# A fused attention and expert-choice kernel: four waits and fills moved to other places

## The chip, the cores and the metric

The kernel runs on one core of a Trainium2 chip. The metric is the time on the device in microseconds (us), the median of several runs.

## The reference, cut to what matters

x has 8 batches of 1024 rows of 256. The kernel computes a row norm of x, attention on it (16 heads of 16, with a second norm, rotary positions, softmax), and a mixture of 8 experts in which each expert takes its best rows; the three are added.

```python
x = L0_attn_x
xn = _layernorm(x, axis=-1)
x = x + _L0_attn_ref(xn, ...) + _L0_ffn_ref(xn, ...)
# attention, on z = norm(xn) * ln_w + ln_b:
scores = einsum('bhqd,bhkd->bhqk', rope(q), rope(k)) / sqrt(hd)
out = einsum('bhqk,bhkd->bhqd', softmax(scores), v)
return xn + out @ Wo.T + bo
# experts: each takes the K = 256 rows of highest affinity of each batch's 1024
gating, index = top_k(softmax(xn @ gate_w).T, K)
h = silu(x_sel @ Wg) * (x_sel @ Wu)
x_out = zeros.at[b_idx, index].add((h @ Wd) * gating)
```

## The kernel before

**Attention.** For each batch b the function attend of every engine walks through 32 cycles of two steps. A step is one group of four heads, one half of the queries and one block of 128 keys. TensorE makes two rows of scores for a step (line 979) into a ring of three buffers, ScalarE takes the exponential of each (line 767), TensorE multiplies the result with the values (line 993). Into the cycles are sown side jobs of TensorE: norm, projections and so on of the next batch, and the output projection ("wo", line 903) of the batch before, in four quarters. In the last batch, which has no next one, the side jobs are those of LAST_JOBS: wo in cycles 9, 15, 23 and 30, "lists" in 27. VectorE takes the top rows of the experts meanwhile, some operations per cycle (TOPS_OF_CYCLE), orders the lists in cycle 26, and copies o_ps out every fourth cycle (line 1436).

**Weights.** An expert's three weights (wg, wu, wd) are loaded by SyncE in load_weights (line 532), all three on one semaphore, w_in. For expert 0 SyncE issues them in the last batch behind its stores of cycle 12. ScalarE casts each to the high part (high_weights, line 736), VectorE subtracts to get the low part (low_weights, line 1367). In the last batch ScalarE makes cast m behind the exponentials of the second step of cycle WEIGHT_CYCLE[m], and VectorE the subtraction in LOW_CYCLE[m]. The wait of a cast is

```python
act.wait_ge(w_in, WEIGHTS * DMA * (e + 1))
```

so each cast waits for all three loads. Casts of later experts stand in the expert units.

**Expert units.** 32 units (8 experts by 4 pairs of batches). GpSimd gathers rows with an indirect DMA (line 666), TensorE turns them (1059), multiplies gate and up (1072) in four blocks f, ScalarE takes silu (751) and a cast (745), VectorE the product (1384) and a subtraction (1376), TensorE the down product (1084), VectorE scales the rows (1399), and GpSimd adds them to the output with an indirect DMA (677). Units 0 and 1 also finish the last batch's attention: quarter_split (lines 1315, 1452, 1454, 1456) and the projections of its quarters. The reciprocals of the softmax sums come from invert (line 1441), which waits for den_in; for the second half of the last batch it stands in unit 0 behind block 1. SyncE writes its result out and spreads it (spread_rec) for unit 1's quarters, behind a load that waits for unit 0's second split.

**The end.** After its last scatter GpSimd waits for the landing of all scatters (line 725), then every engine ends with a DRAIN and an exchange of semaphores (line 113).

**The start.** VectorE sets constants (lines 1551 to 1555), among them ones in the two v_ones buffers, then norms the first half of batch 0 (norm1, norm2, norm3: lines 1121, 1125, 1130), splits the four attention weights (first_weights, line 1563) which ScalarE casts, and so on; GpSimd fills v_ones (set_v, line 647) after const_set has counted minus_half and both memsets. The bound that decides whether scores need a shift (limits) is told to all engines by bound_ready.

Of the kernel before, what the change touches and what calls it, by code (L numbers as in the profile page):

```python
# [19 lines left out]
DMA = 16  # L20
# [96 lines left out]
def program(nc, ctx, g):  # L117
# [4 lines left out]
    ST = SLOTS // P  # L122
    HALVES = CAP // P
    UNITS = NB * HALVES // ST
# [8 lines left out]
    def sb(name, shape, dt=F32):  # L133
        return ctx.enter_context(nc.sbuf_tensor(name, shape, dt))
# [4 lines left out]
    def sem(name):  # L139
        return ctx.enter_context(nc.semaphore(name))  # L140
# [40 lines left out]
    v_ones = [sb(f"v_ones{i}", [P, KT, HPG, KEYS_W]) for i in range(2)]  # L181
# [59 lines left out]
    scattered = [sem(f"scattered{i}") for i in range(UNITS)]  # L241
# [7 lines left out]
    const_set, weights_split, weights_high = sem("const_set"), sem("weights_split"), sem("weights_high")  # L249
# [27 lines left out]
    rotated, sq_ready, v_peaked, bound_ready = (sem(n) for n in ("rotated", "sq_ready", "v_peaked", "bound_ready"))  # L277
# [76 lines left out]
        return qk[:, k, :] if th == 0 else (rec, num)[k // 2][:, k % 2, :]  # L354

    FIRST_BANKS = tuple(score[i][:, w, :] for i in range(RING) for w in range(2)) + (o_ps[:, :], side[:, :])
    WEIGHT_CYCLE = (20, 21, 22)
    LISTS_CYCLE = 26
    LOW_CYCLE = (28, 29, 30)
    END_BANKS = {("wo", q): (q // 2, q % 2) for q in range(QUARTERS)}  # L360
    ROUTER_CYCLE = (9, 19)
    SPLIT_CYCLE, LAST_SPLIT_CYCLE = (7, 8, 17, 18), (7, 8, 14, 18)
# [30 lines left out]
    def hold(eng, s, value):  # L393


        need(eng, s, value)
        if not isinstance(value, int):
            eng.sem_inc(passed, 1)
# [16 lines left out]
    def _(sp):  # L415
# [191 lines left out]
        for e in range(2, E):  # L607
            sp.wait_ge(w_split, WEIGHTS * e)
            load_weights(e)
        hold(sp, y_out, 2 * DMA * NB)  # L610


    @block.gpsimd
    def _(pool):
# [29 lines left out]
        def set_v(b, hg):  # L644

            hold(pool, pv_done, (b * NG + hg - 1) * 2 * KT)
            pool.tensor_copy(v_ones[hg % 2][:, :, :, 0:HD],  # L647
                             v_sb[:, :, hg * HPG * HD:(hg + 1) * HPG * HD]
                             .rearrange("p t (j d) -> p t j d", j=HPG)).then_inc(v_ones_ready, 1)
# [54 lines left out]
        store_xn(0, 0)  # L704
        store_xn(0, 1)
        load_x(1, 0)
        hold(pool, const_set, 3)
        hold(pool, *first_jobs.drained(("v", KT // 2 - 1)))
        set_v(0, 0)
        attend(0, 1, None)  # L710
# [9 lines left out]
        for unit in range(E * UNITS):  # L720
            if unit + 2 < E * UNITS:
                gather(unit + 2)
            scatter(unit)
        for bp in range(UNITS):
            pool.wait_ge(scattered[bp], ST * DMA * E)


    @block.scalar
    def _(act):
# [30 lines left out]
        def attend(b, nxt, prev):  # L760
            for s in range(STEPS):
# [10 lines left out]
                for m in range(WEIGHTS):  # L772
                    if nxt is None and s == 2 * WEIGHT_CYCLE[m] + 1:
                        act.wait_ge(side_free, last_jobs.base)
# [343 lines left out]
    def _(dve):  # L1118
# [41 lines left out]
        def norm3(n, th):  # L1160
            dve.wait_ge(rstd2_done, 2 * n + th + 1)
            if n == 0 and th == 1:
                scaled(late_z, late_xn, mv2, rstd2, z_ready)
            else:
                scaled(z, xn, mv2, rstd2, z_ready)
# [34 lines left out]
        def affinities(n, th):  # L1200
            u = 2 * n + th
            dve.wait_ge(lg_exped, u + 1)
            dve_a.mark(dve.tensor_reduce(lg_sum[:, :], lg_exp[:, :, :], AX_X, ALU.add))
            dve_a.settle(dve)
            dve_a.mark(dve.reciprocal(lg_rec[:, :], lg_sum[:, :]))
            dve_a.settle(dve)
            for t in range(HT):
                last = dve.tensor_scalar(affinity[:, t, th, bass.ds(n * E, E)], lg_exp[:, t, :],
                                         lg_rec[:, t:t + 1], None, ALU.mult)
            last.then_inc(aff_done, 1)  # L1210
# [47 lines left out]
        def limits(bank, n):  # L1258

            dve_f.start(n)  # L1260
            dve_f.mark(dve.tensor_reduce(norms[:, :], bank[0:1, 0:2 * P].rearrange("o (h c) -> o c h", h=2),
                                         AX_X, ALU.max))
            dve.tensor_scalar(terms[:, KEYS_W:KEYS_W + P], bank[0:1, 2 * P:3 * P], LIMIT / VALUE_LIMIT, None, ALU.mult)
            dve.tensor_scalar(terms[:, KEYS_W + P:KEYS_W + 2 * P], bank[0:1, 3 * P:4 * P], -LIMIT / VALUE_LIMIT, None,
                              ALU.mult).then_inc(side_free, 1)
            dve_f.settle(dve)
            dve_f.mark(dve.tensor_tensor(terms[:, 0:KEYS_W], norms[:, 0:KEYS_W], norms[:, KEYS_W:2 * KEYS_W], ALU.mult))
            dve_f.settle(dve)
            to = bound[:, n:n + 1] if isinstance(n, int) else bound[:, bass.ds(n, 1)]
            dve_f.mark(dve.tensor_reduce(to, terms[:, :], AX_X, ALU.max))  # L1270
            dve_f.settle(dve, hold)
            dve_f.mark(dve.tensor_copy(terms[:, KEYS_W + 2 * P:], to))
            dve_f.settle(dve)
            dve.sem_inc(bound_ready, 1)
            dve_f.end()

        def split(n, th, s):
# [17 lines left out]
        def first_low(th, s):  # L1295
            if (th, s) == (1, 0):
                dve.wait_ge(part_out[0], DMA)
                dve.wait_ge(half_turned, 2)
                dve_a.mark(dve.tensor_copy(parts[0][:, 0, :, :], qk[:, 0:2, :]))
                dve_a.settle(dve)  # L1300
            else:
                dve.wait_ge(parts_high, th + s + 1)
            dve.tensor_tensor(parts[s][:, 1, :, :], qk[:, 2 * s:2 * s + 2, :], parts[s][:, 0, :, :], ALU.subtract)\
               .then_inc((q_ready, parts_ready)[s], 1)
# [64 lines left out]
        def turned(unit):  # L1369
            for c in range(DC):  # L1370
                dve.wait_ge(x_high, DC * unit + c + 1)
                dve.tensor_tensor(x_lo[:, c, :], xt_ps[c], x_hi[:, c, :], ALU.subtract).then_inc(x_split, 1)
# [5 lines left out]
        def expert_unit(unit):  # L1378
            e, bp, par = unit // UNITS, unit % UNITS, unit % 2
            for f in range(FC):  # L1380
                dve.wait_ge(silu_done, FC * unit + f + 1)
                dve.wait_ge(up_full, FC * unit + f + 1)
                need(dve, h_split, FC * unit + f - 1)
                dve.tensor_tensor(h[f % 2], u_ps[f % 2], silu[f % 2], ALU.mult).then_inc(h_done, 1)  # L1384
                if f > 0:
                    low(unit, f - 1)
                if unit == 0 and f == 1:
                    invert(NB - 1, 1)
            low(unit, FC - 1)
            if unit + 1 < E * UNITS:  # L1390
                turned(unit + 1)
            if unit < 2:
                quarter_split(NB - 1, 2 * unit)
                quarter_split(NB - 1, 2 * unit + 1)

            need(dve, scattered[(bp - 2) % UNITS], ST * DMA * (e + (bp >= 2)))
            for t in range(ST):
                dve.wait_ge(down_full, ST * unit + t + 1)
                dve.tensor_scalar(y[par][t], rows_ps(t),  # L1399
                                  gates_flat[:, e * COLS + bp * ST + t:e * COLS + bp * ST + t + 1], None, ALU.mult)\  # L1400
                   .then_inc(y_scaled, 1)
            for job in END_JOBS:
                if END_BANKS[job][0] == unit:
                    take(end_jobs, job, None, NB - 1, xt_ps[END_BANKS[job][1]])
            if bp < WEIGHTS and e + 1 < E:
                low_weights(e + 1, bp)
# [32 lines left out]
        def invert(d, qh):  # L1439
            dve.wait_ge(den_in, (2 * d + qh + 1) * DMA)  # L1440
            dve.reciprocal(den_rec[:, :], den[:, :]).then_inc(den_done, 1)
# [50 lines left out]
        def attend(b, nxt, prev):  # L1492
            wide = scores_wide(dve, b)
            jobs = jobs_of(b)
            for c in range(CYCLES):
# [48 lines left out]
                if c in jobs.by_cycle:  # L1544
                    take(jobs, jobs.by_cycle[c], nxt, prev, side[:, :])
                if nxt is None and c in LOW_CYCLE:
                    if c == LOW_CYCLE[0]:
                        dve.wait_ge(parts_out, NB * 2 * PARTS_DMA)
                    low_weights(0, LOW_CYCLE.index(c))

        dve.memset(peaks[:, :], 0.0).then_inc(zeros_set, 1)
        dve.memset(terms[:, :], 0.0).then_inc(zeros_set, 1)
        dve.memset(k_stack[0][:, :, :].bitcast(F32), 1.0).then_inc(ones_set, 1)
        for i in range(2):
            dve.memset(v_ones[i][:, :, :, :], 1.0).then_inc(const_set, 1)

        def first(*job):
            take(first_jobs, job, 0, None, FIRST_BANKS[first_jobs.offset[job] % len(FIRST_BANKS)])

        def first_weights(pair):  # L1560
            dve.wait_ge(weights_high, 2 * pair + 2)
            for i in range(2 * pair, 2 * pair + 2):
                last = dve.tensor_tensor(w_lo[i][:, :, :], raw_weights[i], w_hi[i][:, :, :], ALU.subtract)
            last.then_inc(weights_split, 1)
# [7 lines left out]
        norm2(0, 0)  # L1572
        norm1(0, 1)
        norm3(0, 0)
        first_weights(0)
        norm2(0, 1)
        dve.wait_ge(zeros_set, 2)
# [35 lines left out]
        dve.wait_ge(q_ready, 1)  # L1613
        rotary(0, 0)
        first_low(1, 0)
        affinities(0, 1)
        dve_a.skip(dve, 2 * dve_a.per - dve_a.count)
        dve_a.end()
# [6 lines left out]
        for unit in range(E * UNITS):  # L1625
            expert_unit(unit)
# [41 lines left out]
```

## Time and profile before

| | us |
|---|---|
| runs | 1746.42, 1746.68, 1751.88 (median 1746.68) |
| profiled execution | 1744.11 |
| its span | 1742.3 |
| TensorE busy (matmul) | 1693.1 (97%) |
| ScalarE busy | 1198.2 (69%) |
| VectorE busy | 1031.3 (59%) |
| GpSimd busy | 511.3 (29%) |

The span runs from the first instruction to the last; the execution's time has 1.8 us around it. Busy matmuls overlap and their ends are modelled, so 97% does not say that TensorE is at its peak. The granted clock was 0.992 of full speed over the whole. The last batch's attention lies at about 1028 to 1150 us, the expert units from there to the end.

### The profile page before, as it was taken

The page shows a single profiled execution, that of the slowest core. Times are in us where ns is not written, and L with a number is a line of the kernel's source. Part 1 is how long each engine was busy: PE and PEld are TensorE (multiplying, and loading weights), DVE is VectorE, ACT ScalarE, POOL GpSimd, SP SyncE. Part 2 cuts the span into 40 slices and gives each one's busy share as a digit, 9 for nine tenths or more (in the row PEclk, how much of TensorE's full clock was granted, in tenths as well). Part 3 has the DMA queues.
Part 4 walks back from the last instruction along what each step waited for, and adds up shares of the span by engine and source line. Part 5 has one row for each costly group of instructions (what it writes and reads, how often), then busy time and mean ns, then how long its engine had stood idle before and what let it go on. Part 6 is the DMA issues. An engine that isn't in the chain of part 4 may idle for free.

```text
span 1742.3 us, 28948 instructions
## 1 busy us (share of the span) xinstructions
PE 1693.1 (97%) x11240; PEld 971.8 (56%) x11240; DVE 1031.3 (59%) x2053; ACT 1198.2 (69%) x1419; POOL 511.3 (29%) x479
## 2 busy tenths in 40 slices
PE   6799999999999999999999999999999999999997
PEld 4234344344444434434434433368888888888886
DVE  8664476476457466558547648856455555454543
ACT  5688988888888898898898899963333333343322
POOL 3121121101201111112112100036656565656563
PEclk9899999999999999999999999999999999999998
DMA  4644654764666458456475465445444443535332
GB/s 154 160 110 111 143 106 110 162 121 110 153 128 137 118 130 167 107 131 145 116 157 98 111 147 125 66 143 107 100 91 64 91 89 67 97 61 95 64 56 30
DMA packets 113842, 195.03 MB, mean 112 GB/s; under 512 B 20880, under 2 KB 59664, under 8 KB 113680
## 3 DMA queue, kind: packets, MB, share of 16 engines
q1 hardware_dynamic: 83552, 141.96, 37.0%
q0 software_dynamic: 29040, 49.83, 15.0%
q8 instruction: 106, 1.74, 0.5%
q10 hardware_dynamic: 1088, 1.05, 0.2%
q14 instruction: 56, 0.46, 0.1%
HBM read 116.22 MB, written 76.55 MB: 111 GB/s over the span
## 4 chain that ended last, share of the span: by engine, by line
PE 90%; DVE 4%; DMA 2%; issue 1%; ACT 1%; POOL 1%; SPq 1%; DVEq 0%; ACTq 0%
PE o_ps L993 26%; PE score L1072 20%; PE score L979 19%; PE side L862 5%; PE score L1084 5%; PE o_ps L1084 3%; PE side L872 3%; PE side L1084 2%; PE side L903 2%; PE side L846 2%; PE score L1059 1%; DVE stats L1121 1%; DMA o_sums<-o_sb 1%; DMA probs<-in_wo_t 0%; PE side L853 0%
## 5 line engine op out<-in xcount | busy, mean ns | idle before, releaser
L767 ACT ACTIVATE probs<-score 128x1024 f32<-128x1024 f32 x1024 | 974.3, 1048 | 121.9 <-PE score L979 121.9
L993 PE MATMUL o_ps<-probs,v_ones 128*32 128x512 f32 x4096 | 504.4, 601 | 5.1 <-DVE o_sb L1436 4.8
L979 PE MATMUL score<-q_stack,k_stack 50*128 50x512 f32 x2048 | 407.7, 462 | 5.8 <-issue 3.3
L979 PEld LDWEIGHTS score<-q_stack,k_stack 50*128 50x128 f32 x2048 | 166.2, 185 | 349.6 <-ACT probs L767 295.0
L751 ACT ACTIVATE probs<-score 128x512 f32<-128x512 f32 x128 | 76.6, 598 | 334.3 <-PE score L1072 334.3
L677 POOL DMA_INDIRECT out<-probs,rot x128 | 204.3, 1596 | 212.8 <-DVE probs L1399 183.5
L993 PEld LDWEIGHTS o_ps<-probs,v_ones 128*32 128x32 f32 x4096 | 101.6, 108 | 221.6 <-issue 146.7
L1384 DVE TENSOR_TENSOR probs<-score,probs 128x512 f32<-128x512 f32 x128 | 88.5, 691 | 206.6 <-PE score L1072 179.8
L655 POOL TENSOR_TENSOR square<-qk 128x512 bf16<-128x512 f32 x56 | 77.2, 1407 | 400.1 <-DVE qk L1241 400.1
L1072 PE MATMUL score<-parts,q_stack 128*128 128x512 f32 x640 | 158.3, 390 | 0.0
L666 POOL DMA_INDIRECT qk<-xn_rows,rot x128 | 134.2, 1048 | 38.5 <-issue 29.3
L1072 PE MATMUL score<-parts,zn_hi 128*128 128x512 f32 x512 | 142.5, 395 | 0.1
L1072 PEld LDWEIGHTS score<-parts,q_stack 128*128 128x128 f32 x640 | 119.1, 188 | 23.8
L633 POOL TENSOR_SCALAR ve<-mv 128x4 f32<-128x4 f32 x32 | 8.3, 259 | 357.9 <-DVE mv L1125 357.9
L1072 PEld LDWEIGHTS score<-parts,zn_hi 128*128 128x128 f32 x512 | 95.1, 188 | 23.0 <-issue 0.9
L1436 DVE COPY o_sb<-o_ps 128x512 f32<-128x512 f32 x64 | 44.1, 689 | 104.0 <-PE o_ps L993 104.0
L745 ACT CAST k_stack<-probs 128x512 fp32r<-128x512 f32 x128 | 78.6, 614 | 35.3 <-DVE probs L1384 35.3
L647 POOL COPY v_ones<-v_sb 128x512 f32<-128x512 f32 x32 | 19.7, 615 | 163.3 <-DVE v_sb L1310 85.6
L1376 DVE TENSOR_TENSOR w_hi<-probs,k_stack 128x512 fp32r<-128x512 f32 x96 | 65.5, 682 | 0.0
L1399 DVE TENSOR_SCALAR probs<-score,rot 128x256 f32<-128x256 f32 x64 | 30.8, 483 | 54.0 <-PE score L1084 54.0
L1310 DVE TENSOR_TENSOR v_sb<-side,bv_sb 128x256 f32<-128x256 f32 x56 | 21.1, 417 | 68.8 <-PE side L872 68.8
L1168 DVE COPY xnT<-side 128x512 f32<-128x512 f32 x28 | 19.4, 691 | 47.2 <-PE side L846 47.2
(273 smaller groups left out, 2559.2 us busy)
## 6 DMA issues: line engine op xcount, KB each, us to landing
q_parts<-parts SPq DMA_DIRECT2D x16, 1024.0 KB, 4.4
k_parts<-parts SPq DMA_DIRECT2D x16, 1024.0 KB, 7.3
q_stack<-q_parts SPq DMA_DIRECT2D x62, 256.0 KB, 7.3
k_stack<-k_parts SPq DMA_DIRECT2D x62, 256.0 KB, 9.4
q_stack<-q_parts SPq DMA_DIRECT2D x66, 128.0 KB, 8.1
k_stack<-k_parts SPq DMA_DIRECT2D x66, 128.0 KB, 8.8
o_sums<-o_sb SPq DMA_DIRECT2D x256, 32.0 KB
num<-o_sums SPq DMA_DIRECT2D x32, 256.0 KB
```

The costliest lines, as they stand in the source:

```text
L655: last = pool.tensor_tensor(square[i][:, :], qk[:, i, :], qk[:, i, :], ALU.mult)
L666: pool.indirect_dma_start(xs[par][:, t, :], None, xn_dram[:, :], bass.IndirectOffsetOnAxis(ap=rows_now[bp][:, t:t + 1], axis=0))\
L677: pool.indirect_dma_start(out[:, :], bass.IndirectOffsetOnAxis(ap=rows_now[bp][:, t:t + 1], axis=0), y[par][t], None, compute_op=ALU.add)\
L745: act.copy(h_hi[:, f, :], h[f % 2]).then_inc(h_high, 1)
L751: act.activation(silu[f % 2], g_ps[f % 2], ACT.Silu).then_inc(silu_done, 1)
L767: act.activation(probs[probs_of(b, s)][:, 2 * i:2 * i + 2, :], score[ring_of(b, p)][:, :, :], ACT.Exp, scale=SCALE).then_inc(exp_done, 1)
L862: last = pe.matmul(bank[:, :], wt[:, c, a * P:(a + 1) * P], zt[:, c, th * HALF:(th + 1) * HALF], start=i == 0 and c == 0, stop=i == 2 and ...
L979: last = pe.matmul(score[ring_of(b, p)][:, w, :], k_stack[par][rows, i, kt * P:(kt + 1) * P], q_stack[par][rows, i, qh * HALF:(qh + 1) * H ...
L993: last = pe.matmul(o_ps[j * KEYS_W:(j + 1) * KEYS_W, :], v_ones[par][:, kt, j, :], probs[probs_of(b, s)][:, j, :], start=kt == 0, stop=kt ...
L1072: last = pe.matmul(bank[f % 2], wt[k][w][:, c, f * P:(f + 1) * P], xt[:, c, :], start=i == 0 and c == 0, stop=i == 2 and c == DC - 1)
L1084: last = pe.matmul(rows_ps(t), ht, wt[k][DOWN][:, f, :], start=i == 0 and f == 0, stop=i == 2 and f == FC - 1)
L1384: dve.tensor_tensor(h[f % 2], u_ps[f % 2], silu[f % 2], ALU.mult).then_inc(h_done, 1)
```

## The change

Five edits. (1) The four waits for the scatters move from GpSimd's end to SyncE's end. (2) The last reciprocal moves from the middle of unit 0 behind its last split and the next unit's turned rows. (3) Expert 0's casts move from cycles 20, 21, 22 to 15, 23, 30, and its last subtraction from cycle 30 to 31. (4) The memsets of v_ones leave the start: the first goes behind norm3 of the first half, the second behind the last split of batch 0; GpSimd waits for them one by one. (5) bound_ready is told before a copy instead of behind it.

```diff
-    WEIGHT_CYCLE = (20, 21, 22)
+    WEIGHT_CYCLE = (15, 23, 30)
-    LOW_CYCLE = (28, 29, 30)
+    LOW_CYCLE = (28, 29, 31)
@@ sync
         hold(sp, y_out, 2 * DMA * NB)
+        for bp in range(UNITS):
+            sp.wait_ge(scattered[bp], ST * DMA * E)
@@ gpsimd
+            if b == 0 and hg == 1:
+                pool.wait_ge(const_set, 3)
             pool.tensor_copy(v_ones[hg % 2][:, :, :, 0:HD],
...
-        hold(pool, const_set, 3)
+        hold(pool, const_set, 2)
...
             scatter(unit)
-        for bp in range(UNITS):
-            pool.wait_ge(scattered[bp], ST * DMA * E)
@@ limits
             dve_f.settle(dve, hold)
+            dve.sem_inc(bound_ready, 1)
             dve_f.mark(dve.tensor_copy(terms[:, KEYS_W + 2 * P:], to))
             dve_f.settle(dve)
-            dve.sem_inc(bound_ready, 1)
@@ expert_unit of VectorE
-                if unit == 0 and f == 1:
-                    invert(NB - 1, 1)
             low(unit, FC - 1)
             if unit + 1 < E * UNITS:
                 turned(unit + 1)
+            if unit == 0:
+                invert(NB - 1, 1)
@@ vector, start
-        for i in range(2):
-            dve.memset(v_ones[i][:, :, :, :], 1.0).then_inc(const_set, 1)
...
         norm3(0, 0)
+        dve.memset(v_ones[0][:, :, :, :], 1.0).then_inc(const_set, 1)
         first_weights(0)
...
         first_low(1, 0)
+        dve.memset(v_ones[1][:, :, :, :], 1.0).then_inc(const_set, 1)
         affinities(0, 1)
```

## Rows read from the trace of the kernel before

**Rows 1.** The page, part 4: the chain that ended last, shares by engine.

```profile
PE 90%; DVE 4%; DMA 2%; issue 1%; ACT 1%; POOL 1%; SPq 1%; DVEq 0%; ACTq 0%
```

**Rows 2.** Timeline, ScalarE, last batch (start, busy us, instructions, idle before and releaser).

```profile
1085.68 1.94 ACT L767 ACTIVATE probs<-score 128x1024 f32<-128x1024 f32 x2 [0.20 <-PE score L979]
1087.95 18.44 ACT L767 ACTIVATE probs<-score 128x1024 f32<-128x1024 f32 x20 [0.33 <-PE score L979]
1106.04 1.28 ACT L736 CAST zn_hi<-xin 128x1024 fp32r<-128x1024 f32 x1
1106.97 4.02 ACT L767 ACTIVATE probs<-score 128x1024 f32<-128x1024 f32 x4
```

**Rows 3.** Timeline, SyncE, last batch.

```profile
1079.85 0.47 SPq L532 DMA_DIRECT2D z<-in_wd  x1
```

**Rows 4.** DMA issues of 1070 to 1090 us: count, KB, us from issue to landing.

```profile
z<-in_wd SPq DMA_DIRECT2D x1, 512.0 KB, 16.8
```

**Rows 5.** Timeline, TensorE, last batch.

```profile
1089.01 0.73 PE L979 MATMUL score<-q_stack,k_stack 50*128 50x512 f32 x4
```

**Rows 6.** By tile: the seven loads of wd from 1150 us on.

```profile
DMA to landing us min/median/max: 8.0/8.4/9.8
```

**Rows 7.** Stretches at the start: length, busy PE, PEld, DVE, ACT, POOL, granted clock, DMA.

```profile
45.00:50.00 5.00, 0.00 (x0) 0.00 (x0) 4.97 (x7) 1.04 (x1) 0.61 (x1) 0.68 0.78 171
...
62.00:64.00 2.00, 2.00 (x10) 0.20 (x8) 1.23 (x7) 1.90 (x2) 0.56 (x2) 0.53 0.54 198
64.00:66.00 2.00, 2.00 (x18) 0.71 (x16) 1.26 (x6) 1.35 (x3) 0.71 (x1) 1.00 0.40 111
```

**Rows 8.** Timeline, ScalarE, behind that stretch.

```profile
62.10 1.94 ACT L767 ACTIVATE probs<-score 128x1024 f32<-128x1024 f32 x2 [0.79 <-PE score L979]
64.69 5.61 ACT L767 ACTIVATE probs<-score 128x1024 f32<-128x1024 f32 x6 [0.65 <-PE score L979]
```

**Rows 9.** Timeline, VectorE, last batch, cycles 24 and 26.

```profile
1123.02 0.69 DVE L1436 COPY o_sb<-o_ps 128x512 f32<-128x512 f32 x1 [0.99 <-PE o_ps L993]
...
1133.00 0.35 DVE L1340 TENSOR_SCALAR rot<-rot,row_sb 64x256 f32<-64x256 f32 x1
```

**Rows 10.** Timeline, VectorE, units 0 and 1.

```profile
1164.00 0.55 DVE L1441 RECIPROCAL den_rec<-den 128x64 f32<-128x64 f32 x1 [4.19 <-DMA den<-o_sums]
...
1169.01 0.87 DVE L1315 SCALAR_TENSOR_TENSOR base<-base,grown,bo_sb 128x256 f32<-128x256 f32 x2
...
1190.53 0.87 DVE L1315 SCALAR_TENSOR_TENSOR base<-base,grown,bo_sb 128x256 f32<-128x256 f32 x2
```

**Rows 11.** Timeline, TensorE, the first gate matmuls of units 0 and 1.

```profile
1152.58 0.71 PE L1072 MATMUL score<-parts,zn_hi 128*128 128x512 f32 x2
...
1175.91 0.63 PE L1072 MATMUL score<-parts,zn_hi 128*128 128x512 f32 x2
```

**Rows 12.** The chain of waits at the end (start, us, what).

```profile
1733.40 1.54 POOL out L677
```

**Rows 13.** By line 725 and by line 113: duration ns, first and last start.

```profile
L725 POOLq EVENT_SEMAPHORE  x2: 17/30/43, 1730.8 to 1737.2; - x2
...
L113 POOLq DRAIN  x1: 4646/4646/4646, 1737.4 to 1737.4; - x1
```

**Rows 14.** The chain of waits at the start.

```profile
0.72 4.32 DMA xin<-in_x
...
52.91 0.15 DVE terms L1272
...
70.66 0.59 PE side L846 x4
```

**Rows 15.** Timeline, VectorE, start: first norm, first weight subtraction, batch 1's norm.

```profile
5.40 1.33 DVE L1121 BATCH_NORM_STATS2 stats<-xin 128x6 f32<-128x256 f32 x4
...
16.30 1.29 DVE L1563 TENSOR_TENSOR w_lo<-probs,w_hi 128x512 fp32r<-128x512 f32 x2 [0.59 <-ACT w_hi L808]
...
66.30 1.41 DVE L1121 BATCH_NORM_STATS2 stats<-xn 128x6 f32<-128x256 f32 x4
```

## The prediction

> **What bounds the kernel now.** I read the page's chain first: TensorE holds 90% of it [rows 1]. That share is an average over stages, so I went to the stage of each edit: by timeline for ScalarE and VectorE in the last batch's attention, by time to landing for the weight loads, by timeline for units 0 and 1, by source line for the end, by timeline and chain for the start. In the last batch ScalarE is the bound: 20 exponentials stand in one run of 18.44 us, 0.92 each, without idle time [rows 2], and only cycles with an output projection show it waiting for TensorE: 0.20 before the cycle's second step, 0.33 after the projection. The expert units are bound by TensorE. The two ends are bound by transfers, VectorE and one engine's closing DRAIN.
>
> **1. Expert 0's casts in cycles 15, 23, 30.** A cast stands on ScalarE behind the exponentials of its cycle's second step. Now the three stand in cycles 20 to 22, each moving the next exponential by 0.93 (1106.04 to 1106.97) [rows 2]: 2.79 in all, on the path.
>
> First, when the first cast can start. Cycle 15 is the one whose second step starts at 1085.68 (the run of 20 behind it is steps 32 to 41, and the cast of cycle 20 follows it). Its exponentials end at 1087.62, and there the new cast stands. It waits for w_in at 48, a count that only all three loads of expert 0 together reach. SyncE issues the third, wd, at 1079.85 [rows 3] and it takes 16.8 us to land [rows 4]: 1096.65. Now the cast at 1106.04 comes 9.4 us behind that and never waits. The diff moves no load: SyncE issues them behind its stores of cycle 12. So ScalarE stands still from 1087.62 to 1096.65, **9.03 us**, and all later exponentials are queued behind it. TensorE gets as far as three score buffers allow: one row of scores starts at 1089.01 [rows 5], half of it waits, so it idles from about 1089.4 to 1098.6. VectorE stops at the next copy of o_ps. Nothing else is due in this time, so no other work covers it. The bounds: the other seven wd loads took 8.0 to 9.8 us [rows 6], which gives 1087.85 to 1089.65, a stall of 0.2 to 2.0; the row itself gives 9.03, and I let it vary by 1.5, up to 10.5. I take 9.03, since it is this very transfer behind the same queue of stack loads and broadcast.
>
> The Trainium skill (DMA: Bandwidth & Descriptors, section "Anatomy of one DMA — SWDGE (gpsimd) path") puts a DMA from GpSimd at some 2 us plus its bytes at 436 GB/s; for the three loads, 1.57 MB, that is an estimate of 5.6 us, landing near 1084.5, and the sum would hold no stall. The 16.8 us of [rows 4] speak against it, and the measurement decides; it is a rival below.
>
> Second, TensorE's clock. The trace has one like gap: TensorE did nothing from 45 to 50, the granted clock was 0.68 there on the mean, at the lower level (0.50, 1.2 GHz) until near 64 though matmuls ran again, then 1.00 [rows 7]. ScalarE then waited 0.79 and 0.65 for scores [rows 8]: 1.44 us. A gap of 9.2 us should do the same. Bounds: 0 if the clock stays, and twice as much, 2.9, if it meets ScalarE's pace for longer. I take **1.44**.
>
> Third, the casts themselves. Before, they cost 2.79, and the 0.33 behind the projections of cycles 15 and 30 stands open beside them: 3.45 (the projection of cycle 23 is hidden by the cast of cycle 22). After, each cast covers the 0.33 of its cycle, and the 0.20 of cycle 23 shows again: 2.99. That is -0.46. But VectorE holds 20 top-list operations in cycles 20 to 23, and had only 0.99 of idle time there at 1123.02; the lists' last addition ends at 1133.35 [rows 9], just ahead of the transposes that need it. Cycles 20 to 27 get shorter by 2.79 - 0.93 - 0.20 = 1.66 on ScalarE, VectorE can give back only 0.99, so the lists are some 0.7 late, mostly behind TensorE's slack. I take -0.3 (from -0.46 to +0.3). The subtraction moved to cycle 31 stands where it stood, behind the cycle 30 reciprocal, at no cost.
>
> Part 1: 9.03 + 1.44 - 0.3 = **+10.2**.
>
> **2. Last reciprocal behind unit 0.** VectorE now waits 4.19 us for den, until 1164.00, with three products behind it [rows 10]. Without that, unit 0 runs like unit 1. The first gate matmuls stand at 1152.58 and 1175.91 [rows 11]: 23.33 apart. In unit 1 the first widening of the projection's rows starts at 1190.53, so in unit 0 at 1167.20; the reciprocal, now with its input landed, puts 0.47 ahead of it: 1167.67 against 1169.01 now. From there VectorE's split sets when TensorE does its second projection, so all of it counts: **-1.3**. Nobody needs its result sooner: SyncE takes it up only after the second split. Bounds: 0 (if the load of base, issued behind den's, lands only then) to -1.8 (all waits of TensorE in the unit).
>
> **3. Scatters awaited by SyncE.** The last scatter ends on GpSimd at 1734.94 [rows 12]; GpSimd's wait for it ends at 1737.2; then its DRAIN takes 4.65 us, and the program ends with the exchange behind it [rows 13]. With the wait on SyncE, which has nothing queued behind it, the DRAIN can start at about 1735.15, beside the landing, and ends at 1739.8: **-2.2**. SyncE is through at about 1737.3, long before. Bounds: 0 if the DRAIN itself waits for GpSimd's transfers, -2.3 if the branch ahead of it goes too. I take -2.2, as the row shows it only after everything has landed and yet of full length, so landing isn't what fills it.
>
> **4. The start.** The memsets leave VectorE's way to the first norm, which then waits for x alone: landed at 5.04, so it starts at about 5.06 instead of 5.40 [rows 14, 15], and z ends 0.34 earlier. But VectorE's next work waits for ScalarE's weight casts: idle for 0.59 until 16.30 [rows 15], so z ended at 15.71. Now it ends at 15.37, and the first memset (0.91 and its start) ends at 16.35 to 16.45: +0.1. The second stands behind the last split of batch 0 and pushes the next norm by about 1 us; its xn is complete at 66.30 now and its first user on TensorE starts at 70.66 [rows 14, 15]: hidden, +0, up to 1 if the 4.4 us between them are gone. The bound is told before a copy: this copy of 0.15 and its settling leave the chain [rows 14]: -0.2. Together **-0.1** (-0.5 to +1).
>
> **Sum:** 10.2 - 1.3 - 2.2 - 0.1 = **+6.6 us**. The profiled execution took 1744.11 (span 1742.3 and 1.8 around it), 2.6 below the median of the runs; the sum is a difference and I put it on the median: 1746.68 + 6.6 = **1753.3**.
>
> **Rivals.** *DRAIN stays last:* the wait is hidden, but the DRAIN ends no sooner, 2.2 are not won: 1755.5. For: it is the only long DRAIN. Against: see part 3. Chance 0.20.
> *TensorE becomes the bound behind the gap:* the clock stays low for longer, or the late lists stop TensorE, 3 us more: 1756.5. For: at the start the low clock outlasted the gap by some 9 us. Against: there that cost 1.44. Chance 0.13.
> *The weights are there (not slower):* wd lands after 8.6 us as the others, at 1088.45, because the queue ahead of it is shorter; the stall is 0.8, no gap, no fall of the clock: 0.8 - 0.3 - 3.6 = -3.1, 1743.6. It decides at a landing near 1091.5, where the stall eats the 3.9 of the rest. By the Trainium skill's sum above it would be this one. For: seven of eight loads. Against: the eighth is the one that counts. Chance 0.12.
>
> **How the numbers follow.** The forecast has 0.55; its own range is 1750.5 to 1756. The range 1749.5 to 1758 leaves out the third rival and some tails, 2 in 10. A change under 0.3% (5.2 us) can't be told from none. Of the forecast a quarter lies below that, of the first two rivals nearly nothing; of the third two thirds lie within 0.3%, one third beyond: slower 0.72, same 0.22, faster 0.06.
>
> **What would show it.** Right: a ScalarE wait of 7 to 10 us for wd ahead of the first cast in cycle 15, TensorE idle as long, a granted clock of 0.5 behind it; the reciprocal without wait; a DRAIN on GpSimd from about 2.2 us behind the last scatter's start; the first weight subtraction at about 16.4. Wrong: a cast in cycle 15 that follows its exponential directly, or an end still 7.4 us behind the last scatter.

## The result and the profile after

The changed kernel takes 1758.15 us (median of 8 runs, 1752.59 to 1761.34); the kernel before, run beside it, takes 1748.09 (1746.01 to 1751.88). The ratio is 1.0047, 95% interval 1.0033 to 1.0061: slower by 5.8 to 10.7 us. The profiled execution took 1760.14 (span 1758.3), 16.0 more than the one of before. Line numbers behind the first edits are up to 4 higher, and 1 lower at the start's code near the end of the file. A time given for a kernel is the median of its runs, unless it is said to be that of one execution.

The chain of waits by engine has lost three points of TensorE's [rows 1]:

```profile
PE 87%; DVE 7%; DMA 2%; issue 1%; SPq 1%; POOL 1%; ACT 1%; DVEq 0%; POOLq 0%; ACTq 0%
```

ScalarE's timeline in the last batch, the stretch of [rows 2]: the pair of cycle 15's second step, the new cast, and what follows.

```profile
1085.29 1.94 ACT L769 ACTIVATE probs<-score 128x1024 f32<-128x1024 f32 x2 [0.19 <-PE score L981]
1102.33 1.04 ACT L738 CAST zn_hi<-xin 128x1024 fp32r<-128x1024 f32 x1 [15.09 <-DMA z<-in_wd]
1103.28 3.76 ACT L769 ACTIVATE probs<-score 128x1024 f32<-128x1024 f32 x4
1107.83 1.94 ACT L769 ACTIVATE probs<-score 128x1024 f32<-128x1024 f32 x2 [0.80 <-PE score L981]
1110.85 5.61 ACT L769 ACTIVATE probs<-score 128x1024 f32<-128x1024 f32 x6 [1.08 <-PE score L981]
```

The view ends at 1116, so the last row's group of exponentials is cut there; it goes on. The bracket is the engine's idle time and what ended it. The cast reads xin, which holds wg, but is released by the load of wd into z. The chain there, in order of time and without its pieces of under 0.05 us, shows how long that load was under way; [rows 4] had 16.8:

```profile
1079.52 22.73 DMA z<-in_wd
...
1102.33 0.04 ACT zn_hi L738
```

TensorE's timeline (rows with an idle time) shows two waits where before there was none; the first is for its own stack of keys, not for the cast:

```profile
1091.10 1.22 PE L981 MATMUL score<-q_stack,k_stack 50*128 50x512 f32 x4 [4.05 <-DMA k_stack<-k_parts]
1104.35 0.79 PE L981 MATMUL score<-q_stack,k_stack 50*128 50x512 f32 x2 [9.44 <-ACT probs L769]
```

And windows of 5 us (busy time of each engine with its instructions, then the granted clock, the DMA share, GB/s): at full speed until 1090, at the lower level (0.50, 1.2 GHz) after TensorE had stood still for 4.05 us, still there for some us of full work, up again by 1115, as in [rows 7]:

```profile
1085.00:1090.00 5.00, 2.05 (x16) 1.49 (x12) 3.59 (x8) 2.05 (x3) 0.00 (x0) 1.00 1.03 138
1090.00:1095.00 5.00, 3.81 (x14) 1.02 (x14) 0.00 (x0) 0.00 (x0) 0.00 (x0) 0.54 1.08 272
1095.00:1100.00 5.00, 0.00 (x0) 0.00 (x0) 0.00 (x0) 0.00 (x0) 0.00 (x0) 0.50 1.11 115
1105.00:1110.00 5.00, 5.00 (x24) 0.95 (x22) 2.83 (x7) 3.97 (x5) 0.61 (x1) 0.50 0.58 142
1110.00:1115.00 5.00, 5.00 (x39) 1.51 (x36) 4.83 (x12) 4.16 (x5) 0.00 (x0) 0.92 0.08 20
```

VectorE in unit 0: the last reciprocal has no wait (4.19 in [rows 10]) and the split follows it.

```profile
1186.27 0.54 DVE L1443 RECIPROCAL den_rec<-den 128x64 f32<-128x64 f32 x1
1186.73 0.78 DVE L1317 SCALAR_TENSOR_TENSOR base<-base,grown,bo_sb 128x256 f32<-128x256 f32 x2
```

The end: the last scatter on GpSimd, then by source line (durations in ns, first and last start) the closing DRAINs. GpSimd's now starts while the scatters still run and ends at 1758.09, 5.54 behind the last one's end at 1752.56; in [rows 12, 13] that was 7.14. The last scatter's data has landed at 1754.77, by the trace's semaphore events, and SyncE's wait for it ends there.

```profile
1751.02 1.54 POOL L681 DMA_INDIRECT out<-probs,rot  x1 [0.30 <-issue]
```

```profile
L612 SPq EVENT_SEMAPHORE  x2: 28/28/28, 1737.2 to 1754.8; - x2
L113 POOLq DRAIN  x1: 9717/9717/9717, 1748.4 to 1748.4; - x1
L113 SPq DRAIN  x1: 13/13/13, 1755.0 to 1755.0; - x1
```

The start on VectorE: the first norm now waits for x alone [rows 14, 15]; the memset follows z, and the first subtraction starts without a wait at 16.37, 0.07 later than in [rows 15].

```profile
4.99 1.40 DVE L1123 BATCH_NORM_STATS2 stats<-xin 128x6 f32<-128x256 f32 x4 [1.67 <-DMA xin<-in_x]
15.54 0.91 DVE L1574 MEMSET v_ones<- 128x1024 f32 x1 [0.16 <-issue]
16.37 1.23 DVE L1562 TENSOR_TENSOR w_lo<-probs,w_hi 128x512 fp32r<-128x512 f32 x2
```

**The 16.0 us of the two profiled executions, by stage.** Differences of starts and ends in the two timelines: first exponential of the last batch 0.37 earlier; from there to the pair of cycle 15 nothing (58.30 and 58.29); that pair to the end of the attention 64.95 and 84.33, +19.38; unit 0 (its first product on VectorE to unit 1's) 22.74 and 21.35, -1.39; all other units 0.0; last scatter's end to the end of the span 7.37 and 5.77, -1.60. The +19.4 is more than the median can hold, so the two executions differ in something besides the edits; experiments e10 and e11 show what. Of these 19.4 us, 2.4 are a wait in cycle 30 that no edit explains (see the last section).

### The profile page after: what moved, and what is told of

It reads as the page before. It is cut to its first block, busy times and chain, and to the rows that moved or that the text cites. A ratio compares the mean times of both kernels' runs of the same rounds, so it can differ in the third digit from the quotient of the medians.

```text
span 1758.3 us, 28954 instructions
## 1 busy us (share of the span) xinstructions
PE 1695.8 (96%) x11240; PEld 971.5 (55%) x11240; DVE 1031.1 (59%) x2053; ACT 1198.8 (68%) x1419; POOL 510.5 (29%) x479
## 4 chain that ended last, share of the span: by engine, by line
PE 87%; DVE 7%; DMA 2%; issue 1%; SPq 1%; POOL 1%; ACT 1%; DVEq 0%; POOLq 0%; ACTq 0%
PE o_ps L995 24%; PE score L1074 20%; PE score L981 18%; PE side L864 5%; PE score L1086 5%; PE o_ps L1086 3%; PE side L874 3%; PE side L1086 2%; PE side L905 2%; PE side L848 2%; PE score L1061 2%; DMA z<-in_wd 1%; DVE stats L1123 1%; DVE xn L1132 1%; PE side L855 0%
## 5 line engine op out<-in xcount | busy, mean ns | idle before, releaser
L1074 PEld LDWEIGHTS score<-parts,zn_hi 128*128 128x128 f32 x512 | 95.0, 188 | 23.3 <-issue 1.2
L1170 DVE COPY xnT<-side 128x512 f32<-128x512 f32 x28 | 19.4, 691 | 46.4 <-PE side L848 46.4
```

The lines of the kernel that those rows point to most:

```text
L1074: last = pe.matmul(bank[f % 2], wt[k][w][:, c, f * P:(f + 1) * P], xt[:, c, :], start=i == 0 and c == 0, stop=i == 2 and c == DC - 1)
```

## The experiments

My theory: the new cast of cycle 15 waits for all three loads of expert 0, and that alone is the loss; the other edits together win some 3 us. The rivals: the loss is in the other edits; the cast in its own new place costs time without any wait; the loads are late because of the change.

**e1: the cycles alone.**

```diff
 (the kernel before)
-    WEIGHT_CYCLE = (20, 21, 22)
+    WEIGHT_CYCLE = (15, 23, 30)
-    LOW_CYCLE = (28, 29, 30)
+    LOW_CYCLE = (28, 29, 31)
```

> The kernel before with the casts alone moved (cycles 15, 23, 30, last subtraction in 31). My theory, the first cast waits in cycle 15 for the third load: 7 to 15 us of ScalarE wait, a fall of TensorE's clock behind it, and 10 us slower than before in all (7 to 17; the changed kernel's profiled execution waited 15.1, the runs' median speaks for about 10). Rival, the loss comes from another edit: within 1 us of before.

1757.82 (1755.08 to 1761.55, 6 runs) against 1748.89 (29 runs), ratio 1.0065, interval 1.0043 to 1.0087: slower by 7.5 to 15.2 us. The whole loss is in this edit. ScalarE's timeline and the DMA issue (KB, us to landing) of this kernel:

```profile
1099.24 1.04 ACT L736 CAST zn_hi<-xin 128x1024 fp32r<-128x1024 f32 x1 [10.94 <-DMA z<-in_wd]
1100.20 3.76 ACT L767 ACTIVATE probs<-score 128x1024 f32<-128x1024 f32 x4
1104.76 1.94 ACT L767 ACTIVATE probs<-score 128x1024 f32<-128x1024 f32 x2 [0.80 <-PE score L979]
1106.90 3.77 ACT L767 ACTIVATE probs<-score 128x1024 f32<-128x1024 f32 x4 [0.20 <-PE score L979]
```

```profile
z<-in_wd SPq DMA_DIRECT2D x1, 512.0 KB, 18.0
```

**e2: all but that.** The changed kernel with both lines set back.

> The changed kernel with the casts back in cycles 20 to 22. My theory: no wait of ScalarE for a load in the last batch, and 3.0 us faster than before (2.5 to 3.6): reciprocal 1.3, end 1.6, start 0.1 to 0.4. Rival, the loss lies in the end or the start: slower than before by 5 us or more.

1748.46 (1741.12 to 1750.87, 12 runs), ratio 0.9995 (0.9978 to 1.0012). The loss is gone; a gain of 3 us can't be told from none here (the interval goes from 3.8 us faster to 2.1 slower).

**e3: a semaphore for each load.** The changed kernel, each cast waiting for its own load only.

```diff
+    w_first = [sem(f"w_first{m}") for m in range(WEIGHTS)]
...
-                sp.dma_start(...).then_inc(w_in, DMA)
+                sp.dma_start(...).then_inc(w_first[m] if e == 0 else w_in, DMA)
...
-            act.wait_ge(w_in, WEIGHTS * DMA * (e + 1))
+            if e == 0:
+                act.wait_ge(w_first[m], DMA)
+            else:
+                act.wait_ge(w_in, WEIGHTS * DMA * e)
```

> The changed kernel, but each of expert 0's three loads has a semaphore of its own, and a cast waits for its own load alone. My theory, it is the count of all three that holds the first cast: the wait in cycle 15 falls from 9 to 15 us to what the first load needs, 0.5 to 5 us, and the kernel comes out between 3 us faster and 2 us slower than before. Rival, the queue as a whole is late and the first load lands hardly sooner than the third: the wait stays over 8 us, 7 us slower or more.

1748.91 (1740.79 to 1750.08, 12 runs), ratio 0.9996 (0.9980 to 1.0013). The cast still waits in its traced execution, 5.33 us (5 was expected at the most), but for wg, and TensorE's own late stack stands beside part of that wait (the chain runs through k_stack, landed at 1090.95). wd lands 10.7 us behind wg in this execution (1104.59 against 1093.87), so under the shared count the wait would have been 16 us: two thirds of it are for loads that the cast does not read. ScalarE's timeline and the DMA issues:

```profile
1093.95 1.05 ACT L742 CAST zn_hi<-xin 128x1024 fp32r<-128x1024 f32 x1 [5.33 <-DMA xin<-in_wg]
```

```profile
xin<-in_wg SPq DMA_DIRECT2D x1, 512.0 KB, 13.0
xn<-in_wu SPq DMA_DIRECT2D x1, 512.0 KB, 18.2
z<-in_wd SPq DMA_DIRECT2D x1, 512.0 KB, 22.8
```

**e4: the loads a head group earlier.** The changed kernel; SyncE issues expert 0's loads behind its stores of the last batch's first group.

```diff
             store_o(b, 0)
+            if nxt is None:
+                sp.wait_ge(xn_out, 2 * DMA * NB)
+                sp.wait_ge(side_free, jobs.base)
+                load_weights(0)
             hold(sp, exp_done, b * PAIRS + GROUP_PAIRS)
...
-            else:
-                sp.wait_ge(xn_out, 2 * DMA * NB)
-                sp.wait_ge(side_free, jobs.base)
-                load_weights(0)
```

> The changed kernel, but SyncE issues expert 0's loads in the first group of the last batch (behind its first store of o) instead of behind the stores of cycle 12. My theory: all three have landed long before cycle 15, the wait is gone, the casts cost 0.3 less than before, and the kernel is 3.5 us faster than before (2.5 to 4.2). Rival, the loads now delay the stacks of the next group, and TensorE waits for these: no faster than before, up to 5 us slower.

1744.00 (1740.41 to 1746.50, 12 runs), ratio 0.9977 (0.9961 to 0.9993): faster than both kernels. The cast stands at 1089.12 without a wait. wd lands in about a third of the time (6.5 against 18.0 to 22.8 in e1 and e3), issued where fewer transfers stand ahead of it: SyncE has issued 7 in the 9.3 us before wg, against 16 to 18 behind cycle 12:

```profile
1087.30 1.94 ACT L769 ACTIVATE probs<-score 128x1024 f32<-128x1024 f32 x2 [0.19 <-PE score L981]
1089.12 1.04 ACT L738 CAST zn_hi<-xin 128x1024 fp32r<-128x1024 f32 x1
1091.14 25.77 ACT L769 ACTIVATE probs<-score 128x1024 f32<-128x1024 f32 x28 [0.97 <-PE score L981]
```

The cast itself is followed by a wait of 0.97 us for TensorE, whose stack of keys lands at 1089.99. The loads:

```profile
xin<-in_wg SPq DMA_DIRECT2D x1, 512.0 KB, 4.7
xn<-in_wu SPq DMA_DIRECT2D x1, 512.0 KB, 5.6
z<-in_wd SPq DMA_DIRECT2D x1, 512.0 KB, 6.5
```

**e5, e6, e7: the other edits one by one**, each on the kernel before: the scatters awaited by SyncE; the reciprocal behind unit 0; the start (its edit is the change's own, GpSimd's two waits included, and is not printed again).

```diff
 (e5)
+        for bp in range(UNITS):
+            sp.wait_ge(scattered[bp], ST * DMA * E)
...
-        for bp in range(UNITS):
-            pool.wait_ge(scattered[bp], ST * DMA * E)
 (e6)
-                if unit == 0 and f == 1:
-                    invert(NB - 1, 1)
...
+            if unit == 0:
+                invert(NB - 1, 1)
```

> The kernel before with the four waits for the scatters on SyncE and nothing else. The prediction's theory (the DRAIN starts behind the last scatter and is 4.65 long): the end comes 2.2 us earlier, 5.2 behind the last scatter's end. What the trace of after shows (a DRAIN of about 9.7 that starts while the scatters still run and ends 5.7 behind the last one's end): 1.6 us earlier than the 7.37 of before, whatever else is changed. Rival (DRAIN ends no sooner): 7.4 behind the last scatter. As a time about 1747.2 by the first two, too little to tell from none; the trace decides.

> The kernel before with the last reciprocal behind unit 0's last split and nothing else. My theory: VectorE's wait for den goes, and the first gate products of unit 0 and of unit 1 stand 1.3 to 1.4 us closer (26.38 before between unit 0's first and unit 1's first by the trace, 25.0 then); the end keeps its DRAIN of 4.65. Time 1747.5. Rival (the split then waits for base, so the wait only moves): 26.4 as before, time 1748.9.

> The kernel before with the two memsets moved and the bound told before its copy, nothing else. The prediction: first norm at 5.0, w's first subtraction at 16.4 instead of 16.3, first exponential 0.1 earlier (+0.1, 0, -0.2). The trace of after would have 0.4 (55.31 against 55.70). Rival: the second memset delays xn of the second half and the first exponential comes up to 1 us later. Time 1748.5 to 1748.9, not to be told from none; the first exponential of the trace decides, though it also varies by 0.5 between executions.

Against 1750.59 (31 runs): e5 1745.27, ratio 0.9991 (0.9970 to 1.0012); e6 1749.31, 1.0001 (0.9986 to 1.0016); e7 1752.03, 1.0000 (0.9983 to 1.0017). No time tells any of them from none; the traces do. e5's GpSimd, by source line and at the last scatter: span 1742.4, so the end is 5.8 behind the scatter's end at 1736.65 (e6 and e7, which keep the wait on GpSimd: 7.4). SyncE's wait for the landing ends at 1738.9.

```profile
1735.10 1.54 POOL L679 DMA_INDIRECT out<-probs,rot  x1 [0.30 <-issue]
```

```profile
L612 SPq EVENT_SEMAPHORE  x2: 28/28/28, 1721.3 to 1738.9; - x2
L113 POOLq DRAIN  x1: 9736/9736/9736, 1732.5 to 1732.5; - x1
```

The times of these runs fall into two groups with a gap between them: e5 has six runs from 1743.69 to 1746.09 and four from 1750.44 to 1754.08; the kernel before beside it has 14 up to 1748.40 and 17 from 1750.52 on. These gaps are larger than what any of the three edits wins; the last section has what goes with them.

e6 confirms that the wait for den goes, but not that 1.3 us come of it. By the measure of its expectation (TensorE's first gate product of unit 0 to VectorE's first product of unit 1) it has 25.03 where the first profile of before has 26.38, as expected. But the kernels that keep the reciprocal in its place have 24.88, 24.66, 24.66 and 24.63 where den comes early (e1, e5, e7, e8). From unit 0's first product on VectorE to unit 1's, those six executions took 22.74, 22.34, 21.23, 21.00, 20.98 and 20.96, with waits for den of 4.19, 3.80, 2.71, 0.67, 0.22 and 0.11 (before, e10, e1, e5, e7, e8; the rows of e7 and of e10 below). So VectorE has room for some 2.4 us of waiting, and only what goes beyond it is won; with the move unit 0 takes 21.35 to 22.05 (seven executions), 0.1 to 1.1 more than where the reciprocal stays and den comes early.

```profile
1169.80 0.55 DVE L1443 RECIPROCAL den_rec<-den 128x64 f32<-128x64 f32 x1 [0.22 <-DMA den<-o_sums]
```

```profile
1171.90 0.55 DVE L1441 RECIPROCAL den_rec<-den 128x64 f32<-128x64 f32 x1 [3.80 <-DMA den<-o_sums]
```

e7 has the memset at 15.51 and the first subtraction at 16.41, as predicted; its first exponential stands at 56.03. With the start unchanged it stood between 54.78 and 56.24 (six executions), with the new start between 55.31 and 56.95 (seven): nothing that can be seen.

**e8: what the DRAIN waits for.** e5, and behind the last scatter three power operations of GpSimd into a tile that nobody reads.

```diff
+        for i in range(3):
+            pool.tensor_tensor(late[:, i * HT:(i + 1) * HT], rstd1[:, :], minus_half[:, :], ALU.pow)
```

> e5 with three power operations of GpSimd (about 1 us each, results that nobody reads) behind its last scatter: the closing DRAIN stands behind them. Theory A (the DRAIN ends a fixed time behind GpSimd's last operation): the end comes some 3 us later than in e5, 8.7 behind the last scatter's end. Theory B (it ends a fixed 3.3 behind the landing of the last scatter, as it would for an engine whose transfers are awaited): the end stays at 5.7 behind the last scatter. Time 1750.3 by A, 1747.2 by B.

1750.46, ratio 0.9995 (0.9979 to 1.0011). By its timeline and source line: the powers end at 1744.50, and the DRAIN at 1749.15, 4.65 behind them. That is the 4.646 of [rows 13]. The end is 7.9 behind the scatter, 2.1 later than in e5, where A expected 8.7 and B 5.7. So work behind the scatter does push the end out, as A says, and B is not the whole rule.

Neither is A. The landing of the last scatter is in every trace (the last semaphore event of its DMA). In the seven executions with the wait on SyncE and nothing behind the scatter (after, e2, e3, e4, e5, e9, e11) it comes 2.16 to 2.25 us behind the scatter's end, and the DRAIN ends 5.48 to 5.57 behind that end, but always 3.32 behind the landing, to within 0.001. With the wait on GpSimd (before, e1, e6, e7, e10) the DRAIN ends 4.93 behind the landing; the difference of 1.61 is what the edit wins. In e8 the DRAIN ends 5.47 behind the landing at 1743.68 (SyncE's DRAIN, in the last row below, stands right behind its wait for that landing). What fits all thirteen is the later of two times: 3.32 behind the last landing, and 4.65 behind GpSimd's own last work. That the second holds is shown by e8 alone, and what the DRAIN does in these 3.32 us no run shows.

```profile
1740.92 3.58 POOL L728 TENSOR_TENSOR late<-rstd,minus_half 128x4 f32<-128x4 f32 x3
```

```profile
L113 POOLq DRAIN  x1: 11900/11900/11900, 1737.2 to 1737.2; - x1
L113 SPq DRAIN  x1: 13/13/13, 1743.9 to 1743.9; - x1
```

**e9: early loads, old cycles.** e4 with the casts in cycles 20, 21, 22.

> e4 (the loads issued a group earlier, no wait in cycle 15) with the casts back in cycles 20, 21, 22. It prices the choice of cycles when nothing waits. The prediction's third term: the casts in 15, 23, 30 are worth 0.3 (0.46 on ScalarE, some of it given back by VectorE's lists), so the 64 exponentials of the last batch's second half should take 0.3 to 0.5 longer than in e4's trace, and the time be 1744.3. Rival (the cast hides most of an output projection's cost, all 0.93 of each of the three): 2.8 longer, 1746.8.

1743.77 (1741.43 to 1749.91, 12 runs) against 1747.48 (17 runs), ratio 0.9985 (0.9972 to 0.9998), not to be told from e4's. From the pair of cycle 15 to the attention's end it takes 66.13, e4 65.61: with no load to wait for, the new cycles are worth about 0.5. That is one execution against one, and TensorE's stack, which ScalarE waits for in both (1.54 and 0.97), did not land at the same point in them. The casts' cycles therefore make little of the gain of e4 and e9. Both also have the other three edits, but e2, which has these alone, shows no gain that its runs can tell, and stands 3.4 us behind e4 by the means of their runs, made side by side (1746.94 and 1743.53). So most of the gain is put down to the early loads; the kernel before with early loads and nothing else was not run.

**e10 and e11: both kernels once more.**

> The kernel before, unchanged, for one more profile. Theory (the transfers of the last batch vary between executions, and the profiled execution of before was one of the quick ones): wd's landing anywhere in 16.8 to 23.3, and if it is above 20, ScalarE waits for the stack of cycle 16 some 4 us although no cast stands there; the time then near 1748 to 1750. Rival (the edits make the transfers later): 16 to 18 again and no such wait.

> The changed kernel, unchanged, for one more profile. Theory: the first cast waits until wd has landed, 1.8 to 2.2 behind its 8 us bound at the least: a wait of 9 to 16, by the landing of 16.8 to 23.3; the DRAIN of GpSimd near 9.7 and its end 5.7 to 5.8 behind the last scatter; the 2.4 us wait in cycle 30 of the first profile absent. Rival (the change itself makes this landing late): a wait of 15 again and the 2.4 us wait again.

e10 took 1751.85, e11 1747.20. The kernel before, in e10, has no cast there and still waits: wd lands after 21.6, and TensorE's stack is late as well (it waited 4.13 us for k_stack); that late stack, not wd, is what ScalarE's 4.84 come from.

```profile
1085.92 1.94 ACT L767 ACTIVATE probs<-score 128x1024 f32<-128x1024 f32 x2 [0.19 <-PE score L979]
1092.69 1.94 ACT L767 ACTIVATE probs<-score 128x1024 f32<-128x1024 f32 x2 [4.84 <-PE score L979]
1095.72 1.94 ACT L767 ACTIVATE probs<-score 128x1024 f32<-128x1024 f32 x2 [1.08 <-PE score L979]
```

```profile
z<-in_wd SPq DMA_DIRECT2D x1, 512.0 KB, 21.6
```

The changed kernel, in e11, meets a quick execution; neither theory had so short a landing (11.8), and the wait is 4.68, below the 9 that I expected at the least:

```profile
1092.11 1.04 ACT L738 CAST zn_hi<-xin 128x1024 fp32r<-128x1024 f32 x1 [4.68 <-DMA z<-in_wd]
```

```profile
z<-in_wd SPq DMA_DIRECT2D x1, 512.0 KB, 11.8
```

The stretch from the start of cycle 15's pair to the end of the attention, from the timelines (2.40 of the first profile of after, a wait in cycle 30, taken off):

| | wd lands after | first wait behind the pair | stretch, us |
|---|---|---|---|
| before | 16.8 | 0.33 TensorE | 64.95 |
| before, e10 | 21.6 | 4.84 TensorE | 72.99 |
| all but the casts, e2 | 23.3 | 4.51 TensorE | 71.49 |
| changed, e11 | 11.8 | 4.68 cast | 71.41 |
| casts only, e1 | 18.0 | 10.94 cast | 76.81 |
| changed | 22.7 | 15.09 cast | 81.93 |
| own semaphores, e3 | 22.8 | 5.33 cast | 72.06 |
| early loads, e4 | 6.5 | 0.97 TensorE | 65.61 |
| early loads, old cycles, e9 | 6.2 | 1.54 TensorE | 66.13 |

With the cast in cycle 15 the stretch grows by 10.5 from e11 to the first profile of changed while the landing grows by 10.9: nearly one for one. Without it no cast waits for wd, and what counts is whether the stack is late, which costs 6.5 (e2) to 8.0 (e10); e7 and e8 have the late stack too (waits of 4.16 and 4.36). So the edit costs 6.5 between quick executions (e11 and before), 11.9 between middling ones (e1 and before) and 8.9 between late ones (changed and e10), where the cast's wait runs beside the stack's.

## Why the prediction was right

**Part 1, first step: the stall (9.03).** The mechanism is shown: e1 has it alone, e2 without the cycles has none, and e3 and e4 take it away by two different ways. The size depends on the landing: 10.94 at 18.0 (e1), where the prediction's sum at its 16.8 gives 9.03 and at 18.0 would give 10.2; 15.09 at 22.7; 4.68 at 11.8. I let the landing vary by 1.5; it varied from 11.8 to 23.3. Here the prediction trusted one row of one execution, and that the row lay in the middle is luck.

**Second step: the clock (1.44).** The granted clock fell to 0.50 behind the stall in e1, e3, e11 and the first profile of the changed kernel (windows of 5 us), and was back at full speed by 1115 at the latest. ScalarE waited 0.80 and 0.20 more in e1, 0.80 and 1.08 in the changed kernel (twice) and e3: 1.0 to 1.9 where 1.44 was forecast from [rows 8]. In e10, with no cast there, the late stack brings the same fall and waits of 1.08, 1.07 and 1.07.

**Third step: the casts (-0.3).** The end of the stretch behind the waits (the last 52 exponentials) took 51.82 before and 50.84 in e1, -0.98, where one cast and the 0.33 less the 0.20 make -1.06; the lists cost no more than 0.1. With the cast now in cycle 15 counted (+0.93, less the 0.33 that it covers), that is -0.4, and -0.5 by e4 and e9. The prediction had -0.3.

**Part 1 in sum:** +10.2 predicted at a landing of 16.8; +11.9 measured in e1 at 18.0. The late stack, which costs the kernel before up to 8 us in some executions, was not in the prediction: [rows 2] come from an execution that did not have it.

**Part 2 (-1.3).** -1.39 between the two profiles, but only because den came late in the one of before. Where VectorE waits less than some 2.4 us for den, the move wins nothing and costs 0.1 to 1.1. The step that failed is "all of it counts": it does so only beyond VectorE's slack.

**Part 3 (-2.2).** -1.5 to -1.7 in every execution without work behind the scatter: the end is 5.7 to 5.8 behind the last scatter's end, and was 7.3 to 7.4. The direction is right and the size is not. The step that failed is that the DRAIN stands "beside the landing" from about 1735.15 on and ends 4.65 later, because "landing isn't what fills it". The DRAIN does start early, but it ends a fixed 3.32 behind the landing, so of the 4.93 us behind the landing (0.28 to its start, 4.65 of its own) only 1.61 go. Its full length in [rows 13] did not show that it is free of the landing.

**Part 4 (-0.1).** Not to be seen among starts that vary by 1.5.

**The sum.** +6.6 predicted; 8.2 by the ratio (5.8 to 10.7), 10.1 by the medians. The forecast of 1753.3 stood on 1746.68 for the kernel before; beside the changed kernel that one took 1748.09, and 1758.15 lies 0.15 above the top of the range as written, while 1746.68 with 8.2 more is 1754.9. The rest beyond 6.6 is a stall longer than 9.03 in two of the three traced executions that have it (e1 and the first of changed), and gains of parts 2 and 3 that are up to 1.3 and 0.6 smaller. The late stack, which takes up part of the stall, works the other way. That the sum came so near is partly luck: between pairs of executions the casts' new cycles alone cost 6.5 to 11.9. Two small slips in the prediction change nothing: 1753.3 with 3 us more is 1756.3, not 1756.5, and its shares add up to slower 0.74 and faster 0.04.

**The rivals.** "DRAIN stays last" falls with e5: the end comes 1.6 sooner, not 0; but its ground, a DRAIN that waits for GpSimd's transfers, is part of what the traces show. "TensorE becomes the bound behind the gap" falls: its waits end by 1111, at 1.9 us. "The weights are there" had its own case, a landing after 8.6, in no execution; the shortest was 11.8 (e11). Its turning point, no loss at a stall of 3.9, was set too high. e11 stalls for 4.68, where its sum (no fall of the clock) would give 0.8 slower; against the profile of before, the other quick execution, e11's span is 3.1 longer (1745.4 and 1742.3), and the clock's 1.9 and part 3's 0.6 are what the sum leaves out. e11's time of 1747.20 is that of a quick execution and is not to be set beside the median of quick and late ones.

The Trainium skill (DMA: Bandwidth & Descriptors, section "Anatomy of one DMA — SWDGE (gpsimd) path") gives the estimate of 5.6 us for the three loads, from its fit for DMAs of GpSimd; SyncE issues these. From the first issue all three had landed after 7.5 us in e4, and after 12.8 to 24.2 behind cycle 12 (e11, e2). The same page, section "Queues, rings and completion order", says that each DMA engine takes the descriptors of a ring in their order. e4 against e2, with 7 and 18 transfers issued shortly before, agrees.

## What to carry to other kernels

Before work is moved ahead to where its engine has a gap, ask when its input lands and read that landing in several executions: in one trace it was 16.8, in others 11.8 to 23.3, and the whole verdict hung on it. A wait on a count shared by several loads is a wait for the last of them; a semaphore of its own for the first, or the loads issued one stage earlier, took the loss away, and the latter made the fastest version (0.9977 of before, 0.9961 to 0.9993; not to be told from e9's 0.9985). A wait that an engine has slack for is worth only what goes beyond the slack. And an operation's full length behind a wait does not say what it waits for itself: set its end against each event near it in several executions, and see which distance stays fixed.

## What the runs showed of the hardware

- GpSimd's closing DRAIN takes 4.65 us when all has landed before it starts (before, e1, e6, e7, e10). Started earlier it ends 3.32 us behind the landing of the last scatter (seven executions, within 0.001), or, in e8, 4.65 behind GpSimd's last operation. SyncE's takes 0.013.
- The same transfers of the last batch take very different times from execution to execution (wg 7.7 to 13.9, wd 11.8 to 23.3, issued at the same place), and TensorE's stack comes late in some: it waited 3.1 to 4.1 us for k_stack in six executions (after, e2, e3, e7, e8, e10), not at all in five (before, e1, e5, e6, e11), and 1.1 to 1.5 with the weights issued earlier (e9, e4). The profiled executions of the old cycles without this wait took 1744.11 to 1746.30, those with it 1749.03 to 1751.98; that this is what parts the two groups of times is likely, and not shown for runs without a trace. Why one execution is quick and another late stays open.
- In five of thirteen executions (e5 to e8 and the first of the changed kernel) ScalarE waited 2.4 to 3.2 us for a row of scores in cycle 30, with nothing due from other engines; TensorE waited 2.1 to 2.5 for ScalarE in turn. It is in kernels with and without each edit; its cause is open.
